# Four small graph layers on one core: x by V in the last basis with late signs, the identity product ahead of w, stores by readiness, three layer 0 slots in the turn of the isolated nodes

## The reference, cut to what matters

```python
x   = layernorm(x + L0(x, adj))   # W2 relu(batchnorm(W1 (A_hat x))), batchnorm
x   = layernorm(x + L1(x, adj))   # below
x   = layernorm(x + L2(...))      # graph attention over 256 edges
out = layernorm(x + L3(...))      # two graph convolutions, then LSTMs over windows of 1..4

def L1(features, A, W1, b1, W2, b2):
    ...
    _, U = jnp.linalg.eigh(L_norm)                  # 128 x 128 symmetric
    agg = jnp.einsum('mn,bnd->bmd', U.T, features)
    h = jax.nn.relu(agg @ W1 + b1)
    out = h @ W2 + b2
    return jnp.einsum('nm,bmd->bnd', U, out)
```

## Time and profile before

| | us |
|---|---|
| median of 3 runs (983.03 to 986.38) | 983.21 |
| the profiled execution | 983.05 |
| its span, first to last instruction | 981.2 |
| around the span | 1.85 |
| mean granted TensorE clock over the span | 0.955 |

### The profile page before, as it was taken

How to read it: one execution, slowest core, us unless ns; L and a number is a source line. 1 busy time by engine, 2 the same in 40 slices (tenths; PEclk the granted TensorE clock), 3 DMA queues, 4 the chain that set the end, 5 groups by cost and what they waited for, 6 DMA issues and landing times.

```text
span 981.2 us, 13503 instructions
## 1 busy us (share of the span) xinstructions
PE 900.8 (92%) x4041; PEld 577.1 (59%) x4041; DVE 609.9 (62%) x2143; ACT 609.8 (62%) x1540; POOL 162.3 (17%) x458
## 2 busy tenths in 40 slices
PE   6999968788789987999999999999999999999994
PEld 4565555455566655677776777874444566644442
DVE  6677766657678864666468984335444444444686
ACT  4656647747368862686553456349767788865556
POOL 2334334324333330000000000000000000000065
PEclk9999969979789997999999999999999999999998
DMA  9200000000000000000000000000000000000014
GB/s 268 56 1 1 1 2 1 1 1 2 0 2 1 1 1 1 1 1 1 1 1 1 1 1 1 1 1 1 1 0 1 0 1 1 0 1 0 1 43 129
DMA packets 14329, 13.01 MB, mean 13 GB/s; under 512 B 896, under 2 KB 11056, under 8 KB 14256
## 3 DMA queue, kind: packets, MB, share of 16 engines
q1 hardware_dynamic: 14018, 11.98, 4.4%
q10 hardware_dynamic: 238, 0.16, 0.1%
HBM read 7.89 MB, written 4.19 MB: 12 GB/s over the span
## 4 chain that ended last, share of the span: by engine, by line
PE 71%; DVE 16%; ACT 8%; issue 3%; POOL 1%; DMA 0%; DVEq 0%; ACTq 0%; POOLq 0%
PE bank L982 18%; PE bank L1006 9%; PE bank L844 3%; PE bank L901 3%; PE bank L891 3%; PE bank L834 2%; PE bank L645 2%; PE bank L644 2%; PE bank L573 2%; PE bank L525 2%; PE bank L809 2%; PE bank L969 2%; PE bank L909 2%; PE bank L961 2%; PE bank L798 1%
## 5 line engine op out<-in xcount | busy, mean ns | idle before, releaser
L1489 ACT ACTIVATE hid_t<-bank,gate_b 128x512 f32<-128x512 f32 (+1 forms) x252 | 149.1, 632 | 48.8 <-PE bank L1006 48.2
L1600 POOL TENSOR_SCALAR x<-x,perm 128x128 f32<-128x128 f32 x32 | 29.4, 933 | 575.8 <-DVE perm L2240 575.8
L1006 PE MATMUL bank<-ms,w_t 128*128 128x512 f32 (+1 forms) x288 | 110.8, 528 | 0.1
L982 PE MATMUL bank<-hid_t,w_t 128*128 128x336 f32 (+1 forms) x296 | 106.6, 506 | 1.2 <-DVE x L2215 1.2
L982 PE MATMUL bank<-feat_t,w_t 128*128 128x512 f32 x208 | 93.1, 603 | 0.0
L982 PEld LDWEIGHTS bank<-hid_t,w_t 128*128 128x128 f32 x296 | 55.8, 190 | 46.3 <-issue 25.8
L1006 PEld LDWEIGHTS bank<-ms,w_t 128*128 128x128 f32 x288 | 54.1, 190 | 48.1 <-issue 33.8
L982 PEld LDWEIGHTS bank<-feat_t,w_t 128*128 128x128 f32 x208 | 39.1, 189 | 51.0 <-issue 46.5
L1496 ACT ACTIVATE hid_t<-hid_t 128x512 f32<-128x512 f32 (+1 forms) x72 | 41.8, 581 | 34.8 <-DVE hid_t L2199 25.6
L1276 ACT ACTIVATE pair<-bank,con 128x1 f32<-128x1 f32 x62 | 16.2, 262 | 72.9 <-PE bank L645 72.5
L1085 ACT ACTIVATE x<-x,perm 128x128 f32<-128x128 f32 x128 | 52.3, 482 | 2.6 <-DVE perm L1632 2.6
(11 more groups left out here) (427 smaller groups left out, 2061.6 us busy)
## 6 DMA issues: line engine op xcount, KB each, us to landing
out<-x SPq DMA_DIRECT2D x16, 256.0 KB, 2.6
con<-in_constants SPq DMA_DIRECT2D x1, 449.5 KB, 3.2
feat_t<-in_L_gnn_W SPq DMA_DIRECT2D x2, 128.0 KB, 3.6
e_int<-in_L_gnn_src ACTq DMA_DIRECT2D x1, 128.0 KB
l_w<-in_L_gnn_W SPq DMA_DIRECT2D x2, 64.0 KB
wg<-in_L_gnn_Wg SPq DMA_DIRECT2D x2, 64.0 KB
adj_n<-in_adj SPq DMA_DIRECT2D x1, 64.0 KB, 3.3
x<-in_x SPq DMA_DIRECT2D x4, 0.5 KB, 9.8
```

Of the source, the lines that this page charges most:

```text
L982: return mm(bank[4 * u + BANK_OF[g]][:, 0:w], w_t[:, WB_IH + 4 * (it.p - 1) + g, :], lstm_x(n), start=True, stop=(it.k == 0))
L1006: mm(bank[4 * u + BANK_OF[g]][:, 0:w], w_t[:, WB_HH + 4 * (it.p - 1) + g, :], lstm_h_of(it.chain)[:, 0:w], start=False, stop=True).then_in ...
L1489: f(dst[:, 0:w], bank[4 * u + BANK_OF[g]][:, 0:w], ACT.Tanh if g == G_G else ACT.Sigmoid, bias=gate_b[:, 4 * (it.p - 1) + g:4 * (it.p - 1) ...
L1600: d = pool.tensor_scalar(x[:, t * TB + b, :], x[:, t * TB + b, :], fin_mv[:, t, b, 0:1], fin_rs[:, t, b:b + 1], ALU.subtract, ALU.mult)
```

## The change

- **Identity ahead of w.** `pe_rows` now makes all 128 rows, and right behind it the product of `ident` and A is issued (not in steps 31 and 63). Behind the wait for w come two products of one row each: pv by w and w by pv. pv and w have a tile of their own, `two`; `ident_pv` and its copy go. `filled` into the same bank no longer opens or closes a group.
- **Slots.** `slot_of(step)` adds 3 from step 32 on. Slots 32, 33 and 34 are issued in turn 8: on PE behind levels 0, 2 and 4 of the solve, on ACT behind `act_solve` 0, 2 and 3, on DVE behind `dve_solve` 1, 3 and 4. All later layer 0 work comes three steps earlier.
- **x by V.** The 16 aggregations of layer 1 use V without signs (`l1_ahead`): tile 0 ahead of the second `kept` transposes, tile 1 behind them, tiles 2 to 7 behind the six levels, 8 to 11 in `eigen_signs`, 12 to 15 behind the product that spreads the signs to a row. ACT copies each into `feat_t`. When the signs are known, DVE multiplies tiles 0 and 1 by the sign row and POOL tiles 2 to 15. Layer 1 on PE is then hidden, mid and y.
- **DVE's preparation of layer 2** moves: `edge_sums` to the start of turn 8, `head_strips` between the levels, `soft_masks` to tile 3 of layer 2.
- **Stores.** POOL also normalises tile 11, ACT takes 14 in its place, DVE has 15 only; SP issues in `FIN_ORDER`.

```diff
+FIN_POOL, FIN_ACT, FIN_DVE = (0, 1, 2, 3, 4, 5, 6, 7, 11), (8, 9, 10, 12, 13, 14), (15,)
+FIN_ORDER = (0, 1, 2, 3, 4, 5, 8, 6, 9, 10, 7, 12, 13, 11, 15, 14)
+EXTRA = 3
+ROW_AFTER = 12
+def slot_of(step):
+    if step is None or step < STEPS_BEFORE:
+        return step
+    return step + EXTRA
...
-                mm(h_both[:, k:P], pair[:, h:h + HALF + 1:2], a_sb[:, k:P], start=True, stop=True).then_inc(s["h_rows"], 1)
+                mm(bank[5][:, k:P], pair[:, h:h + 2 * P - 1:2], a_sb[:, k:P], start=True, stop=True).then_inc(s["h_rows"], 1)
+                if h != STEPS_BEFORE - 1:
+                    mm(h_mat[:, k:P], ident, a_sb[:, k:P], start=True, stop=False)
...
                 pe.wait_ge(s["h_w"], h + 1)
-                mm(h_mat[:, k:P], ident_pv, a_sb[:, k:P], start=True, stop=False)
+                mm(h_mat[:, k:P], pv, w_row[:, k:P], start=False, stop=False)
                 mm(h_mat[:, k:P], w_row, pv[:, k:P], start=False, stop=True).then_inc(s["h_rank"], 1)
...
-                filled(384, False)
-                filled(384, False)
+                l1_ahead(0)
                 pe_kept_turned(HALF, 1)
-                filled(128, False)
+                l1_ahead(1)
                 pe_kept_products(HALF, 1)
                 for level in range(6):
                     pe_solve(HALF, 5, level, 6)
+                    l1_ahead(2 + level)
...
+            def l1_ahead(t):
+                if t == 0:
+                    pe.wait_ge(s["x_ready"], CREDIT + TILES)
+                    pe.wait_ge(s["j_v_sb"], SWEEPS + 1)
+                if t > 3:
+                    pe.wait_ge(s["l1_agg_sb"], t - 3)
+                for b in range(TB):
+                    d = mm(l0_last[t % 4][:, b * P:(b + 1) * P], x[:, t * TB + b, :], v_nat, start=True, stop=True)
+                d.then_inc(s["l1_agg"], 1)
...
             def eigen_signs():
+                l1_ahead(8)
                 pe.wait_ge(s["signs_dve"], 1)
                 mm(pa[1][:, 0:2 * len(SPLITS) + 1], v_nat, q_cols[:, :], start=True, stop=True).then_inc(s["basis_pe"], 1)
-                for _ in range(2):
-                    kept_busy()
+                for t in range(9, ROW_AFTER):
+                    l1_ahead(t)
                 pe.wait_ge(s["signs_dve"], 2)
-                tr(ph[0][:, 0:P], u_t[:, :], ident).then_inc(s["basis_pe"], 1)
+                mm(pa[0][:, P:2 * P], ones[:, :], sign_mat, start=True, stop=True).then_inc(s["basis_pe"], 1)
+                for t in range(ROW_AFTER, TILES):
+                    l1_ahead(t)
...
+            def l1_ahead_kept(t):
+                act.wait_ge(s["l1_agg"], t + 1)
+                f(feat_t[:, t * TB:(t + 1) * TB, :], l0_last[t % 4][:, :], ACT.Copy).then_inc(s["l1_agg_sb"], 1)
...
+            pool.wait_ge(s["signs_dve"], SIGNED_ROW)
+            for t in range(SIGNED_DVE, TILES):
+                pool.wait_ge(s["l1_agg_sb"], t + 1)
+                tile = feat_t[:, t * TB:(t + 1) * TB, :]
+                pool.tensor_tensor(tile, tile, s_row.unsqueeze(1).broadcast_to([P, TB, P]), ALU.mult).then_inc(s["l1_pool"], 1)
```

More of the change, by code:

```diff
@@ L423, in _ @@
                 + [(t, "fin_dve", i + 1) for i, t in enumerate(FIN_DVE)]
-            for t, name, count in done:
+            for t, name, count in sorted(done, key=lambda d: FIN_ORDER.index(d[0])):
                 sp.wait_ge(s[name], count)
@@ L549, in beside @@
                 if without_products(slot):
-                    filled(384, slot == HALF - 1)
-                    filled(128, slot == HALF - 1)
+                    last = slot_of(HALF - 1)
+                    filled(384, slot == last, slot not in (STEPS_BEFORE - 1, last))
+                    filled(128, slot == last, slot not in (STEPS_BEFORE - 1, last))
                 for g in TURN_AT.get(slot, ()):
@@ L802, in work, with hidden @@
-                def work(j, next_early):
-                    for u in range(2):
-                        pe.wait_ge(s["l1_agg_sb"], 2 * j + u + 1)
-                        mm(ph[u][:, :], l1_w1[:, :], at[u][:, :, :], start=True, stop=True).then_inc(s["l1_hid"], 1)
+                def hidden(t):
+                    if t < SIGNED_DVE:
+                        pe.wait_ge(s["signs_dve"], SIGNED_ROW + t + 1)
+                    else:
+                        pe.wait_ge(s["l1_pool"], t - SIGNED_DVE + 1)
+                    if t < 2:
+                        pe.wait_ge(s["l1_agg_sb"], TILES - 3 + t)
+                    mm(ph[t % 2][:, :], l1_w1[:, :], feat_t[:, t * TB:(t + 1) * TB, :], start=True, stop=True).then_inc(s["l1_hid"], 1)
@@ L806, in work @@
+                def work(j, next_hidden):
                     for u in range(2):
                         pe.wait_ge(s["l1_hid_sb"], 2 * j + u + 1)
+                        if j == 0 and u == 0:
+                            pe.wait_ge(s["l1_agg_sb"], TILES - 1)
                         for b in range(TB):
@@ L1922, in jacobi_turn @@
                     dve_next(h4)
-                    beside(h4)
+                    beside(slot_of(h4))
             def removal_turn(i):
                 n = STEPS_BEFORE
+                edge_sums()
                 dve_kept_products(n, 0)
@@ L1931, in removal_turn @@
                 dve_solve(n, 0, 1)
+                beside(STEPS_BEFORE + 0)
                 dve_tangents(i)
@@ L2119, in layer2 @@
                         gcn_bias()
+                    if t == 3:
+                        soft_masks()
                     for k in range(2):
```

156 lines of the change are left out of this document (85 added, 71 removed).

## The result

The changed kernel took 967.94 us in the median of its first four runs (967.45 to 970.15) against 984.65 before: ratio 0.9842, 95% interval 0.982 to 0.9863. The forecast was 977.1, so the kernel gained 16.7 us where 7.5 were expected of that median (6.1 of the profiled execution's own time). In four more runs (experiment 5) it took 964.0, 968.2, 972.4 and 980.1 us; the last counts as slow, being over 1.5% above the fastest, and is left out, and with the other three the median is 968.1.

What follows compares the result with a forecast made beforehand. PE was taken to bound about half the steps and layer 1, chains of small operations the other steps, turn 8 and V to layer 1, DMA the end. Terms 6.3 - 5.0 - 1.3 + 3.0 + 1.3 - 8.2 - 2.2 = -6.1 gave 977.1 us, range 967 to 989.

Steps and rivals of the forecast that it cites:

- Identity ahead of w: In the 62 steps: one added product each at 0.43 us, hidden where PE waits for w; +6.3 us, at most 12.5.
- the wide row product: In the steps: loading 128 columns in place of 33 costs nothing, being ahead of POOL's scalars; uncovered, bounded by 6 us.
- The clock among the steps: Added products fill PE's waits, so the clock may stay at 2.4 GHz among the steps: -5.0 us, at most 12 gained.
- Slots: Steps 58, 59 and 60 lose the last layer 0 tiles: -1.3 us, between nothing and 1.9 for three.
- Turn 8: Three slots of layer 0 work added in turn 8: +3.0 us, between -1.1 with the clock up and +7.0 with it low.
- change place only: The shifted slots other than those that leave steps 58, 59 and 60 merely move, with no gain or cost claimed.
- Layer 1: A pair goes from 7.19 to 6.15 us, paced by ACT's root waiting for DVE's statistics: -8.2 us.
- rival 5: In layer 1, POOL's multiplies are held up to twice their time, 7.3 us a pair: 7 us more, 984.1; chance 0.07.
- The stores: At the end, tiles 8, 9 and 10 are stored earlier and the last store ends at 978.1 us: -2.2, bounds -3 and -1.
- From V to layer 1: Last V to layer 1: x by V fits behind the solve's levels, mid(0) +1.3 us; bounds -1 and +11.7.
- rival 4: From 368 to 388 us, x by V runs at 1.2 GHz: +11.7 us, total 988.8; chance 0.12.
- Rival 2: The clock stays up everywhere among the steps and in turn 8: 6.5 and 4.1 us less, 966.5; chance 0.12.

Runs made afterwards that it cites:

- experiment 5: The changed kernel as it is, run again as a base on the chip of the next three runs: 964.02, 968.16 and 972.35 us in the runs that count.
- experiment 1: Changed kernel with the row product at 33 rows and both rank products as before, behind the wait for w: 978.28 us, ratio 0.9931.
- experiment 7: Changed kernel without the three layer 0 slots in turn 8; they stand beside steps 32 to 34 again: 975.42 us, ratio 0.9915.
- experiment 13: Changed kernel with rank and row products as before and without the three slots in turn 8: 975.73 us, ratio 0.9924.
- experiment 10: Changed kernel with six unread 384-column products in TensorE's gaps beside steps 19 and 21 and ahead of step 22: 972.54 us, ratio 0.9872.
- experiment 14: Changed kernel with the identity product issued twice in steps 33 to 62: 970.63 us, ratio 0.9867.
- the square: Medians with rank and row products as before or changed, slots beside steps or in turn 8: neither changed 975.7, slots alone 978.3, products alone 975.4, both 968.1 us.
- experiment 12: Changed kernel with both rank products at 128 rows of weights and ScalarE's layer 1 root queued behind later relus: 957.57 us, ratio 0.9721.
- experiment 6: The kernel before the change with one edit, the row product given 128 rows instead of 33: 980.86 us, ratio 0.9978.
- experiment 3: Changed kernel with the first rank product given 128 rows of weights, 127 of them zero; the second keeps one row: 978.08 us, ratio 0.993.
- experiment 8: Changed kernel with ScalarE's root of a layer 1 pair queued behind the relus of the pair after the next: 963.18 us, ratio 0.9803.
- experiment 11: Changed kernel with the last tiles' engines and the order of the stores as before: 971.5 us in two runs, ratio 0.9866.
- experiment 9: Changed kernel with both rank products given 128 rows of weights, rows 1 to 127 zero: 962.76 us, ratio 0.9783.
- experiment 4: Changed kernel with the row product of 33 rows again instead of 128, identity still ahead of w: 976.31 us, ratio 0.992.

## Why the prediction was wrong

**The step that failed is "Identity ahead of w"**: +6.3 us there, and 0 for the wide row product. It said that one-row weights make the products no shorter "as far as the trace goes". The trace of before already held the gaps of 0.20 us between unequal shapes and 0.11 between equal ones, but I priced a product by a line's busy time over its pairs, 0.43 us, and looked at no distance from start to start. By starts the identity product costs 0.22 us, in 29 steps 6.4 at most and not 12.5; and 22 steps and not 29 found no wait for w in the changed kernel. And the width of the row product is not without effect, it pays for the identity: with 33 columns steps 5, 9, 13 and 17 take 0.23 us more than in experiment 1 (5.39 to 5.42), with 128 they are as long as there within 0.05, and where TensorE waits for w 0.18 us is gained. Over 43 full-clock steps the whole edit gives 3.9 us in place of costing 6.3 (experiment 1); with the clock that goes with it, it gives 10.2 beside the slots and 0.3 without them (experiments 7 and 13).

**"The clock among the steps" was too small and misread.** The direction was right: half clock from 29 us to the last step fell from 68 us to (1 - 0.95) x 2 x 331 = 33. But -5.0 was reasoned from PE's fuller waits. Experiments 10 and 14 fill such waits and change nothing that can be told. What the square shows is that the mean clock of a run is higher, 0.970 to 0.984 against 0.957 to 0.968, where the rank edit and the slots are both in. Which part of the two does it, and why one alone doesn't, is not shown; nor why one kernel gets 0.984 in one run and 0.970 in the next.

**"Slots" and "Turn 8"** together were +1.7 and are -7.3 beside the rank edit (experiment 7), +2.6 without it (experiments 13 and 1). The turn itself cost +5.1 in the profiled run, inside the bounds; over the profiles it takes from 24.8 us at a clock of 0.91 to 30.9 at 0.62 with slots, so in experiment 12 the bound of +7.0 was too low, and 23.4 to 23.9 without.

One term of it was misread: the 1.64 us taken for a product of 512 columns at the lower clock run over the clock's rise at 210.6 us, and in the changed kernel such a product, from its start at 189.69 to the next one's at 191.56, takes 1.87.

The steps hold what the prediction said of them: at the same clock of 0.91 the slots shorten the steps behind turn 8 by 1.8 us (experiment 1 against the kernel before), where -1.3 was forecast, and "change place only" holds for the others. Steps 43 and 44, 6.77 and 7.23 us before and 5.18 and 5.17 in experiment 1, look like a gain, but the batchnorm's root went from step 43 to step 40, which grows by 1.0 to 1.2 us; over steps 40 to 44 together a kernel without slots (experiment 6) takes 26.1 us and one with them (experiment 3) 26.2, both with 6.8 us of half clock.

So the term that failed here is the clock again: the prediction had none for what the slots do to it, and beside the rank edit the whole -7.3 goes with it.

**What held.** Layer 1: the pair 6.10 us against 6.15, the whole -8.1 against -8.2, the root as what holds it (experiment 8), no wait worth naming for GpSimd, rival 5 refuted. A multiply takes 1.27 us and not 1.83. GPSIMD Engine Reference of the Trainium skill, "Key points", speaks of contention between GpSimd and VectorE at their SBUF interfaces; the 1.77 us of the slowest of the 14 is the most that this trace shows of it. The stores: -2.4 against -2.2 (experiment 11), with the last store's data landed 3.2 us behind the last tile. From V to layer 1: levels 1.68 us apart against 1.6, clock 1.00, hidden(0) 22.8 us behind the last V where 21 to 22 were forecast; rival 4 didn't come. These three together, with the small moves around them, are experiment 13: 975.7, 8.8 us below 984.5, where the forecast's own terms give 1.3 - 8.2 - 2.2 = -9.1. So the miss is all in rank products, clock and slots: +3.0 forecast, -7.6 measured. Rival 2 had the right time, 966.5, and an insufficient reason.

## What to carry over

Price an added product by the distance from its start to the next start in the trace, for the weight shapes of both, and not by busy time. A small product between others of 128 x 128 weights should have that shape too, even if rows or columns are zeros that nobody reads (experiments 6 and 9). Where work is moved from one step to another, sum over both: step 43 alone showed a gain of 1.6 us, of which step 40 took most back. When a loop is bound in some steps by one engine and in others by a chain, and the granted clock moves, two edits must be run alone and together: neither's value could be read from the other's run. And where a wait is at the head of an engine's queue, as the root was in layer 1 and the batchnorm's root ahead of a column copy, look at what is ready behind it.

## What the runs showed of the hardware

A pass of a small fp32 product starts 0.111 us behind the one before where both have weights of 128 columns and the same number of rows, whether 65 or 127 columns pass by. With 64 x 64 weights it is 0.06 us; two products of the changed kernel's second solve, 0.12 us from start to start:

```profile
366.26 0.27 PE L683 MATMUL bank<-rot 64*64 64x64 f32 x2
366.38 0.28 PE L684 MATMUL bank<-rot 64*64 64x64 f32 x2
```

Where the weights change between 128 rows and one, the gap ahead of the new product is 0.20 us; the gap inside it, and the first gap after a wait, is 0.21 with 127 columns passing by and falls to 0.16 with 65. Around a product of 33 columns (experiment 4, steps without a wait there) the gap ahead is 0.21, the one inside falls from 0.13 to 0.08, and the one to the next product from 0.20 to 0.15, over the same columns. So the table above holds for one step, and a part of the price of a change of shape gets smaller as the loop goes on.

The weight load of the row product; two lines of it, experiment 4 and the changed kernel (ns min/median/max):

```profile
L652 PEld LDWEIGHTS bank<-u_t,pair x126: 107/110/159, 14.0 to 361.6; 128*33 128x33 f32 x126
```
```profile
L652 PEld LDWEIGHTS bank<-u_t,pair x126: 193/196/337, 13.6 to 350.8; 128*128 128x128 f32 x126
```

The load of 33 columns is 86 ns shorter and yet the step 0.2 us longer. TensorE: Matmul & The Clock Gate of the Trainium skill, section "LDWEIGHTS (loading the stationary operand)", makes the time of a load a matter of its columns and not of its rows; the loads agree (one row takes 184 ns in line 661, 128 rows 196). Its figure gives 28 and 107 ns as estimates for 33 and 128 columns: 79 apart where 86 were measured, but each record, 110 and 196, is 82 to 89 ns longer. The estimate of 107 ns is close to the 0.111 us between passes of one shape, so there the spacing does go with the load; what the step pays for a narrow product is the gaps at the changes of shape.

The kernel with the late root and the equal shapes holds its clock between 0.978 and 0.984 in four runs, and 0.982 to 0.990 with the doubled identity product, where the changed kernel's lay between 0.970 and 0.984 in the seven that count; no experiment tells why.
